# Last stage of an attention and expert block: x added by a DMA with addition, centring and scaling on ScalarE, two wide VectorE operations a group, final products on the turned rows in place

## The reference

```python
xn = layernorm(x)
out = x + attn(xn) + ffn(xn)

def attn(x):
    x = x + token_diffusion(ln(x, ln1_w, ln1_b), Wqk_t, Wv_t, Wo_t, tau_t) * gamma1
    x = x + channel_diffusion(ln(x, ln2_w, ln2_b), Wqk_c, Wv_c, Wo_c, tau_c) * gamma2
    return x

def channel_diffusion(a):               # a: [n, 256] of one batch
    qk, v = (a @ Wqk).T, (a @ Wv).T     # 8 heads of 32 channels
    dot = qk @ qk.T                     # within a head, over the n tokens
    q2 = sum(qk * qk)
    p = softmax((2 * dot - q2[:, None] - q2[None, :]) / sqrt(n) * tau)
    return (p @ v).T @ Wo

def ffn(x):                             # top 1 of 8 experts
    p = softmax(x @ router_W + router_b); e = argmax(p)
    return p[e] * (relu(x @ W1[e] + b1[e]) @ W2[e] + b2[e])
```

## Time and profile before

| | us |
|---|---|
| median of 3 runs | 1318.06 |
| lowest and highest | 1317.38, 1321.65 |
| the profiled execution, its time | 1321.17 |
| the profiled execution, its span | 1319.4 |
| busy in the span: TensorE, ScalarE | 1276.8, 1054.6 |
| busy in the span: VectorE, GpSimd | 476.8, 221.5 |
| mean granted TensorE clock | 0.993 |

### The profile page before, as it was taken

One profiled execution on the slowest core, in us unless ns is written; L12 is line 12 of the kernel. 1 busy time (PEld: TensorE's weight loads), 2 busy tenths in 40 slices (PEclk: granted clock), 3 DMA queues, 4 the chain that ended last, 5 costly groups with the idle time before them and its releaser, 6 DMA issues. The chain is left out here.

```text
span 1319.4 us, 42978 instructions
## 1 busy us (share of the span) xinstructions
PE 1276.8 (97%) x18419; PEld 739.5 (56%) x18419; DVE 476.8 (36%) x1238; ACT 1054.6 (80%) x1182; POOL 221.5 (17%) x310
## 2 busy tenths in 40 slices
PE   6999999999999999999999999999999999998978
PEld 4664334555555555555555555555555555555867
DVE  4764201322322322223223222222222222325987
ACT  5567999888888888888888888888888888882221
POOL 2120650110111110011110101001100110003860
PEclk9898999999999999999999999999999999999999
DMA  5778666456556556465564473555565565733333
GB/s 177 250 207 257 172 178 183 119 144 170 119 124 190 119 120 164 121 148 141 150 143 120 141 161 116 149 150 120 122 181 119 126 176 132 184 141 124 110 95 127
DMA packets 162484, 197.64 MB, mean 150 GB/s; under 512 B 64152, under 2 KB 128664, under 8 KB 158840
## 3 DMA queue, kind: packets, MB, share of 16 engines
q1 hardware_dynamic: 153256, 177.22, 50.1%
q0 software_dynamic: 9040, 17.71, 4.9%
HBM read 154.63 MB, written 35.95 MB: 144 GB/s over the span
## 5 line engine op out<-in xcount | busy, mean ns | idle before, releaser
L968 ACT ACTIVATE shared<-ps 128x1024 f32<-128x1024 f32 x1024 | 970.8, 1038 | 119.8 <-PE ps L1099 119.6
L1122 PE MATMUL ps<-shared,work 128*17 128x256 f32 x7680 | 478.9, 380 | 0.0
L1099 PE MATMUL ps<-mov,stat 52*128 52x512 f32 x2048 | 341.1, 431 | 8.3 <-ACT shared L968 7.1
L990 DVE TENSOR_TENSOR work<-ps,work 128x256 f32<-128x256 f32 x268 | 113.7, 424 | 572.3 <-PE ps L1144 569.2
L1122 PEld LDWEIGHTS ps<-shared,work 128*17 128x17 f32 x7680 | 219.6, 98 | 150.7 <-issue 28.6
L1099 PEld LDWEIGHTS ps<-mov,stat 52*128 52x128 f32 x2048 | 167.0, 185 | 186.5 <-issue 122.1
L1135 PE MATMUL ps<-XNW,work 128*32 128x256 f32 x2496 | 198.5, 390 | 0.3 <-issue 0.3
L1144 PE MATMUL ps<-work,XNW 128*32 128x128 f32 x4992 | 193.0, 273 | 0.0
L1144 PEld LDWEIGHTS ps<-work,XNW 128*32 128x32 f32 x4992 | 149.2, 110 | 52.7 <-issue 0.2
L813 POOL DMA_DIRECT2D y_slots<-work x39 | 22.0, 564 | 584.6 <-DVE work L996 563.5
L1135 PEld LDWEIGHTS ps<-XNW,work 128*32 128x32 f32 x2496 | 51.8, 108 | 108.2 <-issue 101.5
(11 more groups left out here) (168 smaller groups left out, 700.6 us busy)
## 6 DMA issues: line engine op xcount, KB each, us to landing
XNW<-in_L_ffn_W_dram SPq DMA_DIRECT2D x78, 1024.0 KB, 6.2
stat<-q_parts SPq DMA_DIRECT2D x192, 128.0 KB
mov<-q_parts SPq DMA_DIRECT2D x192, 64.0 KB
xg<-in_L_attn_x_dram SPq DMA_DIRECT2D x16, 512.0 KB, 5.0
q_parts<-XNW SPq DMA_DIRECT2D x16, 512.0 KB, 5.6
x_slots<-work SPq DMA_DIRECT2D x1, 4992.0 KB, 16.3
early<-x_slots SPq DMA_DIRECT2D x156, 32.0 KB, 2.2
early<-in_L_ffn_b_dram SPq DMA_DIRECT2D x39, 128.0 KB, 8.0
```

Of the source, the lines that this page charges most:

```text
L968: nc.scalar.activation(probs[:, q % DEEP], ps[:, at:at + 2].rearrange("p a b -> p (a b)"), ACT.Exp, scale=head_scale).then_inc(probs_ready, 1)
L990: ins = nc.vector.tensor_tensor(ysb[:, slot], ps[:, EX, 0:D], ysb[:, slot], ALU.add)
L1099: last = nc.tensor.matmul(ps[:, at + r], stat[rows, head % 2, m * P:(m + 1) * P], mov[rows, head % 2, half * 512:(half + 1) * 512], start= ...
L1122: last = nc.tensor.matmul(ps[32 * j:32 * j + VW, AV, half * 256:(half + 1) * 256], Vh[:, head % 2, m], probs[:, q % DEEP, j * 256:(j + 1) ...
```

## The change

1. `add_x` no longer uses SP's loads, `xg` and GpSimd's arithmetic. GpSimd issues a DMA that adds x from DRAM into `XN`, one for each group, with a semaphore for each (`x_added[G]`), for which `add_expert` waits. All eight loads into `xg` are gone.
2. `make_a2`'s centring and scaling moves to ScalarE: `make_z3`, four activations `scale * XN + bias` a group, with `scale` the `rs1` of the row and `bias` minus mean times `rs1`. For the bias VectorE makes minus the mean (`nm1`, one 128x4 instruction), and GpSimd multiplies it by `rs1` behind its `pow` (`nmr`).
3. `make_a2` is then two VectorE instructions over the whole group of 128x1024: times `l2w`, plus `l2b`.
4. `finals` reads its slices of `a2T` directly; `stage_f` and `a2s` are gone, and the loops over groups 4 to 7 on TensorE, VectorE and ScalarE and both of SP's are written out.

```diff
@@ SP, second and third stage
-                for G in (0, 1):
-                    sp.dma_start(xg[:, G], xt[:, G * GT:(G + 1) * GT, :]).then_inc(x_again[G], 16)
...
-                def load(G, par):
-                    sp.wait_ge(x_added, G - 1)
-                    sp.dma_start(xg[:, par], xt[:, bass.ds(G * GT, GT), :]).then_inc(x_again[par], 16)
...
-                with sp.Fori(0, GROUPS) as G:
+                for G in range(GROUPS):
                     store(G)
@@ GpSimd
                     nc.gpsimd.tensor_tensor(rs1[:, par], ve1[:, par], nhalf[:, 0], ALU.pow).then_inc(rstd3_ready, 1)
+                    pool.wait_ge(rstd3_ready, G + 1)
+                    nc.gpsimd.tensor_tensor(nmr[:, par], nm1[:, par], rs1[:, par], ALU.mult).then_inc(neg_mean3_ready, 1)
...
                     pool.wait_ge(a2_ready, G + 1)
-                    pool.wait_ge(x_again[par], 16 * (G // 2) + 16)
-                    xv = XN[:, G * GT:(G + 1) * GT]
-                    nc.gpsimd.tensor_tensor(xv, xv, xg[:, par], ALU.add).then_inc(x_added, 1)
+                    at = slice(G * GT, (G + 1) * GT)
+                    nc.gpsimd.dma_start(XN[:, at], xt[:, at, :], accum_op=ALU.add).then_inc(x_added[G], 16)
@@ ScalarE
-                def stage_f(G, par):
...
+                def make_z3(G, par):
+                    act.wait_ge(neg_mean3_ready, G + 1)
+                    at_least(act, gram_done, G - 1)
+                    if G >= 2:
+                        act.wait_ge(ring3_ready, use_a2(G - 2) + KC)
+                    for t in range(GT):
+                        last = nc.scalar.activation(a2g[:, par, t], XN[:, G * GT + t], ACT.Identity,
+                                                    bias=nmr[:, par, t:t + 1], scale=rs1[:, par, t:t + 1])
+                    last.then_inc(z3_ready, 1)
...
-                for G in range(GB):
+                make_z3(0, 0)
+                make_z3(1, 1)
+                for G in range(GB - 1):
                     take_a2(G, G % 2)
+                    make_z3(G + 2, G % 2)
+                take_a2(GB - 1, 1)
                 take_gram(0)
+                make_z3(GROUPS - 3, 1)
                 take_t(0)
...
@@ VectorE
                     dve.wait_ge(stats3_step, 2 * G + 2)
+                    at_least(dve, z3_ready, G - 1)
+                    nc.vector.tensor_scalar(nm1[:, par], mv1[:, par, :, 0], -1.0, None, ALU.mult)
...
-                    for t in range(GT):
-                        last = nc.vector.scalar_tensor_tensor(a2g[:, par, t], tile(XN, G, t), mv1[:, par, t, 0:1],
-                                                              l2w[:, :], ALU.subtract, ALU.mult)
-                    last.then_inc(a2_step, 1)
-                    dve.wait_ge(rstd3_ready, G + 1)
+                    dve.wait_ge(z3_ready, G + 1)
+                    nc.vector.tensor_tensor(a2g[:, par], a2g[:, par], over_tiles(l2w), ALU.mult).then_inc(a2_step, 1)
                     dve.wait_ge(a2_step, G + 1)
-                    for t in range(GT):
-                        last = nc.vector.scalar_tensor_tensor(a2g[:, par, t], a2g[:, par, t], rs1[:, par, t:t + 1],
-                                                              l2b[:, :], ALU.mult, ALU.add)
-                    last.then_inc(a2_ready, 1)
+                    nc.vector.tensor_tensor(a2g[:, par], a2g[:, par], over_tiles(l2b), ALU.add).then_inc(a2_ready, 1)
@@ TensorE, finals
-                    pe.wait_ge(staged, G + 1)
...
-                                                        a2s[:, par, c, (2 * k + t) * P:(2 * k + t + 1) * P],
...
+                                last = nc.tensor.matmul(ps[:, FIN[par] + k, t * D:(t + 1) * D], a2T[c][:, at:at + P],
+                                                        mb[:, b, c], start=(c == 0), stop=(c == KC - 1))
```

More of the change, by code:

```diff
@@ L131, in build @@
         nmr = sb("nmr", [P, 2, GT])
+        nm1 = sb("nm1", [P, 2, GT])
         bq = sb("bq", [P, KC])
@@ L1210, in build @@
         a2T.append(take([TOK]))
-        a2s = take([2, KC, GN])
         take_m = views(XN_REST)
@@ L1234, in build @@
         expert_added = sem("expert_added")
-        x_added = sem("x_added")
+        x_added = [sem(f"x_added{G}") for G in range(GROUPS)]
+        z3_ready = sem("z3_ready")
+        neg_mean3_ready = sem("neg_mean3_ready")
         gram_cleared = sem("gram_cleared")
@@ L1253, in build @@
         mb_ready = sem("mb_ready")
-        staged = sem("staged")
         fin_ready = sem("fin_ready")
@@ L1276, in _ @@
                                  ).then_inc(at_loaded[1], 16)
-                with sp.Fori(1, GROUPS // 2) as it:
-                    for par in range(2):
-                        load(2 * it + par, par)
-                with sp.Fori(0, GROUPS) as G:
+                for G in range(GROUPS):
                     store(G)
@@ L1304, in _ @@
                     if G > 1:
-                        add_x(G - 2, G % 2)
+                        add_x(G - 2)
                     for t in range(G * GT, (G + 1) * GT):
@@ L1309, in _ @@
                                                      ).then_inc(gathered, 16)
-                add_x(GROUPS - 2, 0)
-                add_x(GROUPS - 1, 1)
+                add_x(GROUPS - 2)
+                add_x(GROUPS - 1)
             @block.scalar
@@ L1352, in _ @@
                 take_a2(GROUPS - 4, 0)
+                make_z3(GROUPS - 2, 0)
                 take_a2(GROUPS - 3, 1)
                 exp_of(0)
-                stage_f(0, 0)
-                stage_f(1, 1)
+                make_z3(GROUPS - 1, 1)
                 take_a2(GROUPS - 2, 0)
@@ L1362, in _ @@
                 take_t(1)
-                stage_f(2, 0)
                 exp_of(1)
-                stage_f(3, 1)
                 take_r(1)
-                with act.Fori(GB // 2, GROUPS // 2) as it:
-                    for par in range(2):
-                        stage_f(2 * it + par, par)
             @block.vector
@@ L1381, in add_expert @@
                 def add_expert(G, par):
-                    dve.wait_ge(x_added, G + 1)
+                    dve.wait_ge(x_added[G], 16)
                     for t in range(GT):
@@ L1516, in _ @@
                 final(3, 1)
-                with dve.Fori(GB // 2, GROUPS // 2) as it:
-                    for par in range(2):
-                        final(2 * it + par, par)
+                for G in range(GB, GROUPS):
+                    final(G, G % 2)
             @block.tensor
@@ L1610, in finals @@
                         for t in range(2):
+                            at = G * GN + (2 * k + t) * P
                             for c in range(KC):
-                                last = nc.tensor.matmul(ps[:, FIN[par] + k, t * D:(t + 1) * D],
-                                                        a2s[:, par, c, (2 * k + t) * P:(2 * k + t + 1) * P],
-                                                        mb[:, bass.ds(b, 1), c].rearrange("p a n -> p (a n)"),
-                                                        start=(c == 0), stop=(c == KC - 1))
+                                last = nc.tensor.matmul(ps[:, FIN[par] + k, t * D:(t + 1) * D], a2T[c][:, at:at + P],
+                                                        mb[:, b, c], start=(c == 0), stop=(c == KC - 1))
                         last.then_inc(fin_ready, 1)
@@ L1658, in _ @@
                 pe.wait_ge(mb_ready, 2)
-                with pe.Fori(GB // 2, GROUPS // 2) as it:
-                    for par in range(2):
-                        finals(2 * it + par, par)
+                for G in range(GB, GROUPS):
+                    finals(G, G % 2)
 _INS = {"x": "L0_attn_x", "Wqk_t": "L0_attn_Wqk_t", "Wv_t": "L0_attn_Wv_t", "Wo_t": "L0_attn_Wo_t",
```

11 lines of the change are left out of this document (3 added, 8 removed).

## The result

| | before | after |
|---|---|---|
| median, us | 1318.99 (10 runs) | 1325.07 (10 runs) |
| lowest and highest | 1317.38, 1321.65 | 1322.62, 1327.85 |
| ratio, 95% interval | | 1.0041 [1.0026, 1.0055] |
| profiled execution, its time | 1321.17 | 1326.85 |
| profiled execution, its span | 1319.4 | 1323.4 |

The change costs 6.1 us (1325.07 - 1318.99), 0.41%, where 2.7 us less were forecast; 1325.07 lies outside the range of 1312.5 to 1320.0. The two traces put the loss in two places. The smaller is in the last stage, which the prediction worked through. From the first `project` to the end of the span it takes 1323.4 - 1205.60 = 117.8 us, before 1319.4 - 1203.73 = 115.7: +2.1. The larger is a place of which the prediction says nothing: the second head of the second stage, some 1000 us earlier, +5.9.

A forecast was written before the change was run, and what follows sets the result against it. Last stage bound by a chain over VectorE, held up by GpSimd's addition, then TensorE's products. -3.8 (group 7's `gram_of` earlier) - 0.6 (finals) + 1.7 (clock) = -2.7 us: 1315.4 against median 1318.06; range 1312.5 to 1320.0.

The forecast's parts named there:

- Two x loads that leave SP: On SP ahead of the load of AT: they lie under the head loop, so their removal gains nothing.
- The issue of a DMA: On GpSimd, each group's accumulating DMA of 512 rows: issue taken as 0.8 us, ends 0.52 and 2.26.
- the high end (2.26): GpSimd's DMA issue if every 128 rows cost a whole issue; as a rival 1319.5 to 1321 us, chance 0.10.
- the added stations eat the gain: Rival: multiply of 0.7 us and issue of 1.1 delay group 6 by 3.9 us; 1317.5 to 1318.5, chance 0.10.
- The break-even of 1.8: On GpSimd: about 1.8 us a DMA issue is where the last stage's gain is used up.
- The other stations: Last stage, per group: GpSimd's multiply with wait 0.32 us, ScalarE's `make_z3` 2.15, VectorE's two wide operations 2.5.
- TensorE would not wait within its block: Last stage: groups 1 to 3 ready 0.6 to 1.0 us ahead, TensorE without a wait, block ending at 1258.7 us.
- The clock: TensorE's `product_m` and `gram_of(7)`: 3.4 us at half speed after pauses, +1.7 us, bounds 0 and 3.4.
- no fall: Rival, the forecast's nearest neighbour: TensorE's clock does not fall, all else as forecast; 1313.7 us, chance 0.30.
- Finals in place: Last products on TensorE: loop goes, 14.09 us against 4 x 3.45 and a 0.34 us pause; -0.6 us, bounds 0 and -0.7.
- The choked queue: Rival: last gathers behind six accumulating DMAs in GpSimd's queue land 15.5 us late; about 1331 us, chance 0.15.
- the point of 5.0: GpSimd's queue: 5.0 us for each accumulation is the point from which the choked queue decides.

The follow-up runs named there:

- e13: The kernel before with an unused tile of 128 bytes a partition; ratio 1.0034.
- e1: The kernel before with only the new 32-byte tile `nm1` declared, unused, so later tiles move by 32 bytes; 1325.2 us, ratio 1.0047.
- e4: The kernel before with only the addition of x done by GpSimd's accumulating DMA, all x loads gone, no added tile; 1315.16 us, ratio 0.9974.
- e8: The kernel before with the DMA addition and the last products in place, centring and scaling left on VectorE; 1312.80 us, ratio 0.9963.
- e3: The kernel before with only the last products read in place and the loops over groups 4 to 7 written out; 1318.81 us, ratio 1.0004.
- e6: The changed kernel, `nm1` moving no tile, with DMA additions 0 to 5 issued behind `rstd(7)`, ahead of the last four gathers; 1322.87 us, ratio 1.0037.
- e12: The changed kernel, `nm1` moving no tile, with all eight DMA additions issued behind the last four gathers; 1316.10 us, ratio 0.9977 to before.
- e16: The kernel before with the unused 32-byte tile, the row of zeros moved 224 bytes further to a multiple of 256 again; ratio 1.0000.
- e2: The changed kernel with `nm1` taken from the last stage's own area, so that no tile moves; 1319.42 us, ratio 1.0007 to before.
- e14: The kernel before with an unused tile of 256 bytes a partition; ratio 0.9998.
- e7: The kernel before with an unused tile of 64 bytes a partition; ratio 1.0038.
- e10: The kernel before with the unused 32-byte tile and VectorE's three operations on the last small loads moved behind the first head's `norm_o`; 1316.28 us, ratio 0.9983.
- e15: The kernel before with no new tile, only the row of zeros and the small tiles behind it moved by 32 bytes; ratio 1.0044.

## Why the prediction was wrong

**Two x loads that leave SP: nothing.** True, but the list of what the change does ahead of the last stage stopped there. The step that failed most is this omission: a new tile was priced at nothing, without a word, and moving the row of zeros off a multiple of 256 bytes costs 4.5 to 6.2 us (0.0034 in e13 to 0.0047 in e1, of 1319), most or all of the 6.1 measured. No rival had it. The trace of before couldn't have given its size; that tiles move, and that the longest DMA of SP's queue reads from one, could have been read.

**The issue of a DMA, 0.8 us.** This is the term of the last stage that was mis-sized. It ended 1.46 us behind the multiply, over four issues 4 x 0.66 = 2.6 us more than forecast. The gathers with the pauses ahead of them, the longer one behind the issue among them, took 32.3 us in six rounds for 6 x 5.17 = 31.0, 1.3 more; `pow` and multiply took 1.33 us for 1.38, over seven groups 0.3 less. So the multiply of group 6 ended at 1259.67 - 1.87 = 1257.80 us on before's clock, 3.5 us behind the forecast 1254.3. The reasoning "rows hardly count" came from 32 and 128 rows, 519 and 564 ns, which are one and the same to within 0.05 us; for 512 rows with addition it fell. Whether the rows or the addition make the issue longer, no run tells. With its pause (1.56) the truth lies half way between the forecast and the high end (2.26). Of the rivals written down "the added stations eat the gain" was nearest: it had group 6 late by 3.9 us, but through a multiply of 0.7 us, which took 0.19. The break-even of 1.8, reckoned without the clock, held: less the 1.8 us that `product_m` lost at half clock, group 7's `gram_of` would have come 0.4 us earlier than before.

**The other stations** were sized well: multiply 0.19 and a gap of 0.1 (0.32), `make_z3` 2.1 (2.15), wide operations 2.5 (2.5). `make_a2(6)` ended at 1264.36, 1262.5 on before's clock, only 0.5 us earlier than before, and `take_r(0)` behind `make_z3(7)` and two copies, as written, put `product_m` 1.5 us later. So group 7's `gram_of`, forecast at -3.8 (-2.1 with the clock's fall), came at +1.4. That TensorE would not wait within its block failed too: 0.58 us before group 3's `gram_of` and 1.82 before `product_dots(0)`, since `take_t(0)` stands behind `make_z3(5)`; the prediction followed `take_r` past `make_z3`, not `take_t`.

**The clock, +1.7 us.** The mechanism was right, the fall hit `product_m` and `gram_of(7)`. It lasted longer: it cost 1.8 us on `product_m` (3.78 - 1.99) and some 1.2 on `gram_of`, whose first matmuls show 1.06 us in place of 0.60 to 0.70. Say 3.0, inside the bounds 0 and 3.4. e4 and e8, too, have `product_m` at half clock, so the neighbour "no fall" was never there.

**Finals in place, -0.6 us.** The 64 matmuls took 14.08 us, as before; only the pause ahead of them fell, from 1.08 in e4 to 0.78 here. -0.3, and in e3 nothing that can be measured.

**The choked queue** cost nothing. The addition's DMA of 512 KB landed in 6.3 us (median) where a plain load took 3.8, but VectorE waited only 0.43 us for a gather ahead of `final(0)`. In e4, which came there earlier, it waited 1.91, and the end still came 45.0 us behind group 7's `gram_of`, before 45.2.

```profile
1278.92 1.67 DVE L1381 SCALAR_TENSOR_TENSOR XNW<-shared,gate,XNW 128x256 f32<-128x256 f32 x4 [0.43 <-DMA shared<-y_slots,pos_u]
```
```profile
XNW<-in_L_attn_x_dram POOLq DMA_DIRECT2D x8, 512.0 KB, 6.3
```

e6 gives the size: six additions and four gathers took from 1263.14 to 1285.70 us, with 0.95 us a gather and 1.4 for the first issue some 2.9 us an addition, an estimate. It lies under the point of 5.0. The Trainium skill ("Collectives: The Full Stack", section "The bandwidth ceiling: the fold count and why AG ≠ RS ≠ AR") tells of a collective whose DMAs add that the second source read halves the rate. Against 1.7 us, the low end of a plain copy in the earlier trace rows, 2.9 is 1.7 times as long, near that rule.

In sum for the stage: forecast -2.7, measured +2.1; GpSimd's rounds explain 3.5 of the 4.8 us missed, the longer fall of the clock 1.3 and the finals 0.3, together 5.1. e12, with the issues off GpSimd's rounds and the tile where it moves nothing, took 1316.1 us for the forecast 1315.4; that is near by luck in part, since the forecast had 0.8 us an issue in those rounds and less of the fall of the clock.

## What to carry to other kernels

List what a change declares as well as what it executes: a new tile moves all that stand behind it, and here the cure is to keep one row on a multiple of 256 bytes (e16), or to put the tile where it moves nothing (e2). Take a change with several parts apart: of these, the DMA addition alone (e4), with or without the finals (e8), beats both kernels, and the ScalarE part gives it all back (e2) unless the issues leave GpSimd's rounds (e12). When an engine comes round just in time, price everything put on its queue by the number of rounds ahead of the first reader, and follow each copy that is moved past, not only the one you look at.

## What the runs showed of the hardware

- A DMA of 4992 packets of 1 KB, all read from one row of 1 KB in each partition of SBUF, landed in 16.3 us where that row began at a multiple of 256 bytes (before, e14, e16 and every kernel that left it there), and in 17.4 to 17.5 us at 32, 64 or 128 bytes behind one (the changed kernel, e1, e7, e10, e13, e15).
- Issuing an accumulating DMA of 512 rows of 1 KB from GpSimd's queue held GpSimd for 1.32 to 1.45 us, and 0.30 more ahead of a gather; a plain one of 128 rows 0.56.
- Beside GpSimd's 128x1024 addition small VectorE operations took longer too, not only large ones: a 128x4 one 2.08 us in place of 0.17. With the addition gone (e4) two of TensorE's three waits for `make_a2` went.
- The first 32 `project` matmuls of the last stage took 7.17 us in some profiled executions and 8.8 to 8.9 in others, behind a pause of 2.4 us. These 1.7 us are not any change's: of kernels with before's last stage, e1, e13 and e16 show the one, e7, e14 and e15 the other.
